# Routed experts placed in the steps of the selective scan, head inputs in another order of stages, side pieces of the column softmax in quarters

## The reference

```
# A: Mamba block; D_INNER 256, D_STATE 16
def step(hstate, ins):
    x_t, dt_t, B_t, C_t = ins
    dA = jnp.exp(dt_t[..., None] * A)
    hstate = hstate * dA + (dt_t * x_t)[..., None] * B_t[:, None, :]
    y_t = jnp.einsum('bdn,bn->bd', hstate, C_t)
    return (hstate, y_t)
...
y = (jnp.swapaxes(ys, 0, 1) + x * D_skip) * jax.nn.silu(z)
hidden = residual + y @ out_proj_w
ff = jax.nn.silu(hn @ gate_w) * (hn @ up_w) @ down_w      # hn = rms(hidden), 512 wide
# F: 32 experts of width 64, top 8 per token, and one shared expert
h = jax.nn.silu(flat @ wg.T) * (flat @ wu.T)
acc = acc + w[:, None] * (h @ wd.T)
```

## Time and profile before

| | |
|---|---|
| Median of 3 runs | 7267.65 us (7259.87 to 7271.13) |
| The profiled execution | 7271.85 us |
| Its span | 7270.1 us |
| PE busy | 5207.4 us, 72% |
| DVE busy | 5160.6 us, 71% |
| ACT busy | 3896.3 us, 54% |
| POOL busy | 1562.8 us, 21% |

### The profile page before, as it was taken

One profiled execution on the slowest core, in us unless ns is written; L12 is line 12 of the kernel. 1 busy time (PEld: TensorE's weight loads), 2 busy tenths in 40 slices (PEclk: granted clock), 3 DMA queues, 4 the chain that ended last, 5 costly groups with the idle time before them and its releaser, 6 DMA issues. The chain is left out here.

```text
span 7270.1 us, 82198 instructions
## 1 busy us (share of the span) xinstructions
PE 5207.4 (72%) x23371; PEld 1824.1 (25%) x23371; DVE 5160.6 (71%) x6074; ACT 3896.3 (54%) x5386; POOL 1562.8 (21%) x983
## 2 busy tenths in 40 slices
PE   5466677978854868833333367777775999999999
PEld 2122233433311222200000111111112344444443
DVE  4688845444455666489798489999994688888887
ACT  4333321242444534689799489999993333333333
POOL 0244400000011000000000000000000577777776
PEclk7678788988967988955555689999997999999999
DMA  0000000000003112000000233332331110111110
GB/s 17 4 0 0 0 13 12 0 15 0 0 16 106 34 29 51 17 11 0 13 0 0 73 36 41 38 43 36 44 36 21 44 30 21 24 30 30 30 30 12
DMA packets 204967, 174.58 MB, mean 24 GB/s; under 512 B 145346, under 2 KB 186446, under 8 KB 196526
## 3 DMA queue, kind: packets, MB, share of 16 engines
q1 hardware_dynamic: 204606, 170.09, 12.4%
HBM read 118.80 MB, written 51.23 MB: 23 GB/s over the span
## 5 line engine op out<-in xcount | busy, mean ns | idle before, releaser
L1964 DVE TENSOR_REDUCE cs_neg<-cs_s_ps 128x1 f32<-128x1024 f32 x1024 | 1182.4, 1215 | 112.2 <-PE cs_s_ps L1831 96.1
L1885 ACT ACTIVATE cs_E<-cs_s_ps,cs_neg 128x1024 f32<-128x1024 f32 x1024 | 1134.4, 1120 | 135.9 <-DVE cs_neg L1964 135.9
L2237 ACT ACTIVATE da_P<-da_P 128x1024 f32<-128x1024 f32 x512 | 541.2, 1057 | 930.9 <-DVE da_P L2312 912.1
L2278 POOL TENSOR_TENSOR da_psum<-da_psum,da_P 128x1024 f32<-128x1024 f32 x384 | 904.9, 2357 | 366.7 <-ACT da_P L2237 334.0
L2295 DVE TENSOR_REDUCE da_mx<-da_s_ps 128x1 f32<-128x1024 f32 x512 | 623.9, 1220 | 198.2 <-PE da_s_ps L2161 198.1
L1831 PE MATMUL cs_s_ps<-cs_q,cs_k 64*128 64x512 bf16 x2048 | 390.5, 396 | 372.2 <-ACT cs_E L1885 343.6
L1259 PE MATMUL hypb_o_ps<-hypb_P,hypb_vq 128*32 128x512 f32 (+3 forms) x640 | 193.7, 933 | 607.5 <-DVEq L1649 403.6
L2312 DVE TENSOR_TENSOR da_P<-da_s_ps,da_lift 128x1024 f32<-128x1024 f32 x512 | 600.6, 1215 | 3.5 <-PE da_s_ps L2165 3.4
L2161 PE MATMUL da_s_ps<-da_k,da_q 64*128 64x512 f32 x2048 | 553.1, 618 | 20.8 <-DMA da_v<-vf 15.2
L1842 PE MATMUL cs_r_ps<-cs_E,cs_w 128*32 128x512 f32 x4096 | 551.5, 613 | 1.4 <-POOL cs_w L1924 1.4
L2175 PE MATMUL da_o_ps<-da_P,da_v 128*64 128x512 f32 x2048 | 495.9, 605 | 0.0
(11 more groups left out here) (437 smaller groups left out, 8904.0 us busy)
## 6 DMA issues: line engine op xcount, KB each, us to landing
da_q<-qf SPq DMA_DIRECT2D x32, 512.0 KB, 8.7
da_k<-kf SPq DMA_DIRECT2D x32, 512.0 KB, 10.6
cs_q<-q_parts SPq DMA_DIRECT2D x384, 32.0 KB
cs_k<-k_parts SPq DMA_DIRECT2D x384, 32.0 KB
qf<-cs_side_sb SPq DMA_DIRECT2D x32, 256.0 KB, 3.4
kf<-cs_side_sb SPq DMA_DIRECT2D x32, 256.0 KB, 5.3
vf<-cs_side_sb SPq DMA_DIRECT2D x32, 256.0 KB, 5.8
da_v<-vf SPq DMA_DIRECT2D x16, 512.0 KB, 11.9
```

Of the source, the lines that this page charges most:

```text
L1885: act.activation(E[:, seg.slot(t, E_RING), h, :], s_ps[:, seg.slot(u, RING, 2), :], ACT.Exp, bias=neg[:, g, j, h:h + 1], accum_out=z[:, g, ...
L1964: dve.tensor_reduce(neg[:, g, j, h:h + 1], s_ps[:, seg.slot(u, RING, 2), :], AX.X, ALU.max, negate=True).then_inc(maxed, 1)
L2237: act.activation(P[:, g % RING, :, :], P[:, g % RING, :, :], ACT.Exp).then_inc(exped, 1)
L2278: pool.tensor_tensor(psum[:, :, :], psum[:, :, :], P[:, g % RING, :, :], ALU.add).then_inc(pooled, 1)
```

## The change

- The loop over the 16 states now runs over 8 segments of 512 tokens, written out for 16 states. In each step it carries a block of two routed experts for the same 512 tokens, with lags of 1 to 3 steps: gate, factors (up and the spread weight) and down on PE; on ACT the sigmoid as Exp, Ln, Exp and a copy of the gate, from the table that the decays use; its product with the gate on POOL; two multiplies on DVE. The sum over the blocks stays in PSUM for the segment and is copied over dt. Buffers for dtx, gate, sigmoid and hid lie in x, which is loaded again with load_f.
- DVE takes both scans of a step one behind the other, keeps the carries later, and takes a segment's output during the next segment's first step.
- The routing stands ahead of `mamba` with a load of the router alone; the experts' weights are loaded with the selectors. The shared expert becomes a fifth block of the feed-forward. `add_in_place` adds two tensors.
- Head inputs: rings of 6 and 5 for a and time, other lags and another order within a slot, on ACT, DVE and POOL.
- Column softmax: the side pieces are made in quarters of 128 columns, 1, 1 and 2 of them behind three tiles in a row (3 to 5, 7 to 9, 11 to 13); the copy on ACT comes in the tile of the last; the collect comes one score later; q and k are cleared on the quadrants that need it, q by DVE and k by POOL.

The diff, cut to what is new in the scan (its removed lines are the function above) and to the lines that differ elsewhere:

```
@@ -429,126 +426,242 @@
+def scan_with_experts(nc, dt, xs, zs, bc, bc_sel, A, D_skip, ident, scratch, xn, W, sel, wT):
+    NSEG, NE = S // CH, D_STATE
+    SEGS, LAST = B * NSEG, B * NSEG - 1
+        dtx, gate_sb, sig, hid = (scratch[:, 2 * i * CH:2 * (i + 1) * CH].rearrange("p (k c) -> p k c", c=CH) for i in range(4))
+        b_ps, c_ps, y_ps = sc.ps("b_ps", [128, CH]), sc.ps("c_ps", [128, CH]), sc.ps("y_ps", [128, 2, CH])
+        g_ps, u_ps, w_ps, o_ps = (sc.ps(n, [128, CH]) for n in ("g_ps", "u_ps", "w_ps", "o_ps"))
...
+                def spread(g, n):
                     wait(pe, b_used, u(g, n) + 1)
...
+                    pe.matmul(b_ps[:, :], bc_sel[:, n * 128:(n + 1) * 128], bc[:, now(g)], start=True, stop=True).then_inc(b_ready, 1)
+                    wait(pe, c_copied, blk(g, n) + 1)
+                    pe.matmul(c_ps[:, :], bc_sel[:, (D_STATE + n) * 128:(D_STATE + n + 1) * 128], bc[:, now(g)],
+                              start=True, stop=True).then_inc(c_ready, 1)
+                def add_up(g, n):
                     for k in range(2):
                         wait(pe, hc_ready, u(g, n, k) + 3)
...
+                        if n == 0:
                             wait(pe, y_taken, g * 2 + (k + 1))
...
+                        pe.matmul(y_ps[:, k, :], ident, hC[:, k, :], start=(n == 0), stop=(n == D_STATE - 1)).then_inc(hc_used, 1)
+                def gate(g, n):
+                    wait(pe, gate_taken, blk(g, n) * 2 + 2)
+                    pe.matmul(g_ps[:, :], W["gate"][:, n * 128:(n + 1) * 128], xn[:, now(g)], start=True, stop=True).then_inc(gate_ready, 1)
+                def factors(g, n):
+                    wait(pe, hid_done, blk(g, n) + 2)
+                    pe.matmul(u_ps[:, :], W["up"][:, n * 128:(n + 1) * 128], xn[:, now(g)], start=True, stop=True)
+                    pe.matmul(w_ps[:, :], sel[:, n * 128:(n + 1) * 128], wT[:, now(g)], start=True, stop=True).then_inc(factors_ready, 1)
+                def down(g, n):
+                    wait(pe, hid_done, blk(g, n) + 3)
+                    if n == 0:
+                        wait(pe, out_free, g + 1)
+                    pe.matmul(o_ps[:, :], W["down"][:, n * 128:(n + 1) * 128], hid[:, n % 2, :], start=(n == 0),
+                              stop=(n == NE - 1)).then_inc(down_done, 1)
+                def emit(g):
+                    spread(g, 0)
+                    for n in range(NE):
+                        if known(g, n, 1):
+                            add_up(*at(g, n, 1))
+                        if n + 1 < NE:
+                            spread(g, n + 1)
+                        if known(g, n, 2):
+                            factors(*at(g, n, 2))
+                        gate(g, n)
+                        if known(g, n, 3):
+                            down(*at(g, n, 3))
+                emit(0)
+                with pe.Fori(1, SEGS) as g:
+                    emit(g)
...
             @block.scalar
             def _(act):
...
+                act.sem_inc(gate_taken, 2)
+                act.preload_act_table_set("natural_log_exp_and_others")
+                def decays(g, n):
+                    for k in range(2):
+                        wait(act, scanned, u(g, n, k) + 1, act_waits)
+                        act.activation(dA[:, k, :], dt[:, k, now(g)], ACT.Exp,
+                                       scale=A[:, n + k * D_STATE:n + k * D_STATE + 1]).then_inc(decay_ready, 1)
+                    wait(act, c_ready, blk(g, n) + 1)
+                    wait(act, hc_ready, u(g, n) + 2)
+                    act.activation(c_sb[:, :], c_ps[:, :], ACT.Copy).then_inc(c_copied, 1)
+                def sigmoid(g, n):
+                    wait(act, gate_ready, blk(g, n) + 1)
+                    wait(act, hid_done, blk(g, n) + 1)
+                    act.activation(sig[:, n % 2, :], g_ps[:, :], ACT.Exp, scale=-1.0).then_inc(gate_taken, 1)
+                    act.activation(gate_sb[:, n % 2, :], g_ps[:, :], ACT.Copy).then_inc(gate_taken, 1)
+                    wait(act, gate_taken, blk(g, n) * 2 + 4)
+                    act.activation(sig[:, n % 2, :], sig[:, n % 2, :], ACT.Ln, bias=1.0).then_inc(logged, 1)
+                    wait(act, logged, blk(g, n) + 1)
+                    act.activation(sig[:, n % 2, :], sig[:, n % 2, :], ACT.Exp, scale=-1.0).then_inc(sig_done, 1)
+                def emit(g):
+                    for n in range(NE):
+                        decays(g, n)
+                        if known(g, n, 1):
+                            sigmoid(*at(g, n, 1))
...
             @block.gpsimd
             def _(pool):
...
+                def weigh(g, n):
+                    lasting(c_copied, blk(g, n) + 2)
+                    for k in range(2):
+                        lasting(scanned, u(g, n, k) + 3)
+                        lasting(hc_used, u(g, n, k) + 1)
+                        pool.tensor_tensor(hC[:, k, :], h[:, k, :], c_sb[:, :], ALU.mult).then_inc(hc_ready, 1)
+                def silu(g, n):
+                    lasting(sig_done, blk(g, n) + 1)
+                    pool.tensor_tensor(gate_sb[:, n % 2, :], gate_sb[:, n % 2, :], sig[:, n % 2, :], ALU.mult).then_inc(silu_done, 1)
+                def emit(g):
+                    for n in range(NE):
+                        weigh(g, n)
+                        if known(g, n, 1):
+                            silu(*at(g, n, 1))
...
             @block.vector
             def _(dve):
...
+                def inputs(g, n):
+                    wait(dve, b_ready, blk(g, n) + 1)
                     for k in range(2):
...
+                        dve.tensor_tensor(dBx[:, k, :], dtx[:, k, :], b_ps[:, :], ALU.mult).then_inc(b_used, 1)
+                def scan(g, n, k, fresh):
+                    wait(dve, b_used, u(g, n, k) + 2)
+                    wait(dve, decay_ready, u(g, n, k) + 1)
+                    wait(dve, hc_ready, u(g, n, k) + 1)
+                    if not fresh:
+                        wait(dve, carried, u(g, n, k) - 2 * D_STATE + 1)
+                    state = carry[:, n + k * D_STATE:n + k * D_STATE + 1]
+                    dve.tensor_tensor_scan(h[:, k, :], dA[:, k, :], dBx[:, k, :], 0.0 if fresh else state,
+                                           ALU.mult, ALU.add).then_inc(scanned, 1)
+                def keep(g, n, k):
+                    wait(dve, scanned, u(g, n, k) + 3)
+                    dve.tensor_copy(carry[:, n + k * D_STATE:n + k * D_STATE + 1], h[:, k, CH - 1:CH]).then_inc(carried, 1)
+                def times_up(g, n):
+                    wait(dve, silu_done, blk(g, n) + 1)
+                    wait(dve, factors_ready, blk(g, n) + 1)
+                    dve.tensor_tensor(gate_sb[:, n % 2, :], gate_sb[:, n % 2, :], u_ps[:, :], ALU.mult).then_inc(up_done, 1)
+                def times_weight(g, n):
+                    wait(dve, up_done, blk(g, n) + 1)
+                    if known(g, n, 2):
+                        wait(dve, down_done, blk(g, n) - 1)
+                    dve.tensor_tensor(hid[:, n % 2, :], gate_sb[:, n % 2, :], w_ps[:, :], ALU.mult).then_inc(hid_done, 1)
...
+                def emit(g, fresh):
+                    for k in range(2):
+                        dve.tensor_tensor(dtx[:, k, :], dt[:, k, now(g)], xs[:, k, now(g)], ALU.mult).then_inc(dtx_done, 1)
+                    wait(dve, dtx_done, g * 2 + 2, dve_waits)
+                    for n in range(NE):
+                        inputs(g, n)
+                        scan(g, n, 0, fresh)
+                        scan(g, n, 1, fresh)
+                        keep(g, n, 0)
+                        if known(g, n, 2):
+                            times_up(*at(g, n, 2))
+                        keep(g, n, 1)
+                        if known(g, n, 2):
+                            times_weight(*at(g, n, 2))
+                        if n == 0 and known(g, n, 1):
+                            take_output(g - 1)
+                        if n == 2 and known(g, n, 3):
+                            take_experts(g - 1)
+                for b in range(B):
+                    emit(b * NSEG, True)
+                    with dve.Fori(b * NSEG + 1, (b + 1) * NSEG) as g:
+                        emit(g, False)
...
         norm(nc, "ln0", x, xn, C["ones"], C["eps5"])
...
+        with Scope(nc, "l0") as sc:
+            wT = sc.sb("wT", [96, T], BF16)
+            route_experts(nc, xn, C, ident_b[:, :], io, wT)
+            mamba(nc, x, xn, C, io, wT)
...
+def route_experts(nc, xn, C, ident_b, io, wT):
     p = PACKS["e"]
     with Scope(nc, "moe") as sc:
...
+        router, w = sc.sb("router", [128, NE0]), sc.sb("w", [128, NT, NE0])
+        at = p.at["router"][0]
+        load(nc, "load_router", [(router[:, :], io["pack_e"][:, at:at + NE0])])
+        route_groups(nc, xn, router[:, :], C["tri8"], w[:, :, :])
         spread_weights(nc, "spread0", w[:, :, :], NE0, wT, ident_b)
...
-        a, time, f = (sc.sb(n, [128, 4, CH]) for n in ("a", "time", "f"))
```

(52 more changed lines are left out.)

214 lines of the change are left out of this document (78 added, 136 removed).

## The result

The changed kernel takes 6920.33 us, median of 4 runs (6918.44 to 6926.59), against 7263.76 (7249.16 to 7271.13) for the kernel before in the same runs: a ratio of 0.9531, with a 95% interval from 0.9514 to 0.9548. The forecast was 6957 in a range from 6875 to 7085. The profiled execution has a span of 6919.2 us, 350.9 less than the one of before.

A forecast was written before the change was run, and what follows sets the result against it. DVE was taken to carry the scan and PE alone the experts, so one was laid into the other. Layer 0 -211, head inputs -35 and column softmax -65 gave -311: 6957 us from a 7267.65 median, range 6875 to 7085.

The forecast's parts named there:

- The scan step: Scan with experts: period 5.7 from turns of POOL and scans, plus 0.15 for register waits: 5.85 us, bounds 5.3 to 6.5.
- T + 3.1 to 3.3: Scan step: when DVE is ready for the next scan, T being the end of the step's second scan.
- The loop branches: Scan stage: six loop branches with written-out bodies were to cost 12 us (0 to 25).
- The tail: End of the scan: the last expert block runs alone through ACT, POOL, PE and DVE, 8 us.
- The rest of layer 0: Layer 0 beside the scan: experts' loop and load removed, loads, addition and shared expert added; layer 0 in sum -211 us.
- Head inputs: Head-input stage: DVE's 5.3 and about 1 behind POOL give a 6.4 us period, 16 to fill and drain: 118, -35.
- Column softmax: Column softmax: quarters fit between scores except 0.15 behind the last, 60 us, and the later collect 5: -65.
- The clearing: Column softmax: clearing q and k in quadrants by two engines was to change 0 us (-2 to +4).
- The first rival, copies held by POOL: Scan step: carry copies take turns with POOL, period 6.7, +115 us, 7072; chance 0.20, including another wait of that size.
- Fully hidden silu and experts: Rival in the scan step: silu and experts hide wholly, period 5.3, -70 us, 6887; chance 0.11.
- PE at half clock: Rival in the scan: PE's 4.96 becomes 9.9 us a step, +518 us, 7475; chance 0.04.
- The side edits without effect: Rival: the head-input and column softmax edits don't do what they say, +100 us, 7057; chance 0.06.

The follow-up runs named there:

- no_silu: The changed kernel without POOL's multiply of gate and sigmoid in the scan: 6842.8 us, ratio 0.9414 to the kernel before.
- scan_alone: The changed kernel with all work of the routed experts left out of the scan: 6787.3 us, ratio 0.9338 to the kernel before.
- b_in_place: The changed kernel with the second dtx and B product put back in B's PSUM bank and scanned there: 6852.0 us, ratio 0.9437 to the kernel before.
- cs_halves: The changed kernel with each column softmax side piece made in two halves behind two tiles, not quarters behind three: 6925.3 us, ratio 0.9536 to the kernel before.
- cs_only: The kernel before with the new column softmax alone: 7248.4 us, ratio 0.998; its last stretch, with no line changed, took 1797.6 us.

## Why the prediction held, step by step

- The scan step: right, with its mechanism. 5.79 for 5.85; turns of POOL and scans set it (no_silu, scan_alone, b_in_place). Of the 0.15 us for waits on register values at most 0.07 were there (3.5 + 1.07 + 1.15 is 5.72), and DVE's readiness, T + 3.1 to 3.3, was T + 2.5; as it lay inside silu it cost the sum nothing, but I mis-sized the next limit by it: DVE alone needs 4.97, not the 5.3 of my lower bound.
- 128 steps of 5.79 are 741 us; the stage has 45.4 more, where I had 64. Segment follows segment 97.65 us apart (434.1 to 1020.0 in six), 5.0 above 16 steps, for my 5.5; the first takes 90.4, 2.2 below 16 steps. The loop branches, 12 in the sum, cost nothing that shows: DVE has no wait on issue in the stage. The tail is 12.6 for 8: 7 x 5.0 - 2.2 + 12.6 = 45.4. This is 19 of the 27 us by which the scan beat the forecast; 8 are the shorter step.
- The rest of layer 0: load_sel +9.6 for +9.5, load_f +6.7 for +5.7, routing with its load -10.4 for -8.4, the feed-forward and the addition +28.2 for +25. Right to 3 us each. In all -235.9 for -211.
- Head inputs: the stage took 117.4 for 118, but by luck, as two errors that cancel. Its period is 6.98, not 6.4, and filling and draining takes 5.7, not 16. Two steps of it on DVE and POOL (the rows that answer to the earlier trace rows): POOL's first subtractions start 6.99 apart, and beside POOL an instruction of DVE that needs 0.69 takes 1.24 and another 1.65, together 1.5 where I had about 1.

```profile
1901.30 1.15 POOL L1213 TENSOR_TENSOR hi_t_rest<-hi_time,hi_t_parts 128x512 f32<-128x512 f32 x1 [2.05 <-ACT hi_t_parts L1154]
1901.76 1.24 DVE L1177 TENSOR_TENSOR hi_a<-hi_a,hi_turned 128x512 f32<-128x512 f32 x1
...
1904.78 1.62 POOL L1217 TENSOR_TENSOR hi_t_parts<-hi_t_rest,hi_t_parts 128x512 bf16<-128x512 f32 x1 [2.33 <-ACT hi_t_parts L1160]
...
1905.29 1.65 DVE L1198 TENSOR_TENSOR hi_rest<-hi_a,hi_parts 128x512 f32<-128x512 f32 x1
...
1908.29 1.15 POOL L1213 TENSOR_TENSOR hi_t_rest<-hi_time,hi_t_parts 128x512 f32<-128x512 f32 x1 [1.90 <-ACT hi_t_parts L1154]
```

- Column softmax: -60.6 for -65, and 1272.2 for the 1264 that the stage was to take (3 of these 8 us are the ends of the stretches, see above). Here too two sizes were wrong and all but cancel: the waits for scores fell by 45 us, not 60, and those for the head's result, by the later collect, by 15, not 5 (22.5 before, one of 7.7 after). Of the scores' 29.5 that are left I had 15, as 0.15 behind each last quarter; cs_halves, with 8 us more of these waits and 2 us more of the stage, neither shows nor excludes such a price. The clearing, taken as 0: POOL needs 7.06 us for k, the first load comes 3.2 us later and the first score 1.1 sooner after the start of the stage, 23.4 for 24.5.
- The first rival, copies held by POOL, fell in its term: the one-column copies take 0.13 us in the mean of 256. It stood in its mechanism for wide operands: the 128-column copy takes 1.19. The Trainium skill, "SBUF — State Buffer", section "SBUF: two separate sides", has the port pair held against a DVE operation in a two-port mode or with two SBUF inputs; the scans agree, held with two SBUF inputs and not held from PSUM (1.25), and so does the 128-column copy, if it runs in such a mode. Whether a copy of one column does, that section doesn't say, and no row shows the mode. I gave the rival 0.20 with a row for wide operands only, and that doubt was right.
- Fully hidden silu and experts, 5.3: no; silu's turn of 1.24 us is on the path, and 0.75 of it come back without it before the next limit is reached. PE at half clock: no, 0.98. The side edits without effect: no in this kernel; but cs_only shows how near that was, by a way that I had not thought of, the place of a loop's instructions.
- The forecast was 311 us less, the two traces lie 350.9 apart. Of these 40 us 25 are in layer 0, 20 in two attention passes that vary by as much between executions, 4 in layer 2 ahead of them, 1 elsewhere, less 5 in the last stretch and 4 in the column softmax.

## What to carry to other kernels

Where DVE and POOL both read SBUF, count turns instead of busy time: the sum of the operations that take turns is a floor, and moving one input of one of them to PSUM, even in place in the bank that another operand came in, takes it out of that sum. Work that lies in the PSUM and PE time of such a step comes nearly for nothing, so choose for it the form with the fewest SBUF-to-SBUF operations. Before an edit is judged by its whole time, compare the stages in which no line is changed: here one of them moved by 47 us.
